# Layer 2's rows by expert: one scatter of every row, or a gather block by block through an index table

## What is computed

```python
xn = layernorm(x)                        # 2048 rows of 512
# attention: in each of the 512 columns l the 8 batches attend to each other
q = transpose(xn, (2, 0, 1))             # (l, batch, position c)
s = xn + transpose back(softmax(q q^T / sqrt(256)) q)
# mixture of experts: 8 experts, 2 per row, F = 800
probs = softmax(xn @ gate_w.T)
top_vals, top_idx = top_k(probs, 2); top_vals /= sum(top_vals)
h1, h3 = xn @ w1[e].T, xn @ w3[e].T
y = sum over the two experts of top_vals * ((silu(h1) * h3) @ w2[e].T)
x = x + s * silu(y)
```

## Time and profile before

| | us |
|---|---|
| median of 3 runs | 1500.8 (1498.28 to 1501.86) |
| the profiled execution | 1501.16, its span 1499.2 |
| PE busy | 1349.1 (90%) |
| DVE busy | 699.4 (47%) |
| ACT busy | 565.9 (38%) |
| GpSimd busy | 615.0 (41%) |
| attention of layer 1 | about 167 to 760 |
| across_batch | about 761 to 875.5 |
| experts | 875.6 to about 1445 |
| combine | about 1446 to the end |

### The profile page before, as it was taken

How to read it: one execution, slowest core, us unless ns; L and a number is a source line. 1 busy time by engine, 2 the same in 40 slices (tenths; PEclk the granted TensorE clock), 3 DMA queues, 4 the chain that set the end, 5 groups by cost and what they waited for, 6 DMA issues and landing times. The chain is left out here.

```text
span 1499.2 us, 24968 instructions
## 1 busy us (share of the span) xinstructions
PE 1349.1 (90%) x7870; PEld 1149.3 (77%) x7871; DVE 699.4 (47%) x1617; ACT 565.9 (38%) x1775; POOL 615.0 (41%) x516
## 2 busy tenths in 40 slices
PE   6989899999999999999877579999999999999940
PEld 6934487878787878888547469999999999999930
DVE  6352376666676766666447332223222222232237
ACT  3421276655556656666534221212212111122124
POOL 0020155444444545454325445172662617451135
PEclk9889999999999999999878689999999999999985
DMA  8035720000000000000015566273772728555247
GB/s 290 1 84 143 277 93 15 15 14 14 14 14 14 14 25 17 14 14 15 7 58 177 195 225 187 99 247 109 238 243 96 268 72 289 171 169 182 72 126 258
DMA packets 67068, 171.47 MB, mean 114 GB/s; under 512 B 6448, under 2 KB 15040, under 8 KB 66704
## 3 DMA queue, kind: packets, MB, share of 16 engines
q0 software_dynamic: 25776, 98.73, 19.9%
q1 hardware_dynamic: 35632, 61.95, 12.9%
q10 hardware_dynamic: 5616, 10.23, 1.9%
HBM read 125.26 MB, written 45.61 MB: 114 GB/s over the span
## 5 line engine op out<-in xcount | busy, mean ns | idle before, releaser
L1681 PE MATMUL bank<-expert_weights,rows_t 128*128 x1872 | 359.4, 347 | 1.8 <-DVE rows_t L1613 1.6
L1681 PEld LDWEIGHTS bank<-expert_weights,rows_t 128*128 128x128 f32 x1872 | 340.8, 189 | 5.8 <-issue 2.6
L958 ACT ACTIVATE room<-bank,room 128x256 f32<-128x256 f32 (+1 forms) x512 | 208.9, 415 | 114.0 <-DVE room L891 113.9
L986 POOL TENSOR_TENSOR room<-room 128x1024 f32<-128x1024 f32 (+1 forms) x128 | 187.9, 1468 | 120.1 <-DVE room L868 120.1
L742 PE MATMUL bank<-room 96*128 (+2 forms) x1024 | 189.1, 327 | 0.0
L1625 DVE TENSOR_TENSOR x_keep<-x_keep,bank 128x400 f32<-128x400 f32 x78 | 44.5, 571 | 304.2 <-ACT x_keep L1568 302.9
L1093 POOL TENSOR_TENSOR expert_weights<-x_keep,expert_weights 128x1600 fp32r<-128x1600 f32 (+2 forms) x49 | 160.2, 3270 | 54.9 <-DMA expert_weights<-w 54.6
L742 PEld LDWEIGHTS bank<-room 96*128 96x128 f32 x1024 | 159.1, 191 | 13.7 <-issue 0.4
L1704 PE MATMUL bank<-expert_weights,act_t 128*128 x702 | 165.6, 389 | 1.0 <-ACT act_t L1573 1.0
L993 POOL TENSOR_TENSOR room<-room 128x256 f32<-128x256 f32 x128 | 93.2, 728 | 173.5 <-DVE room L932 172.2
L1704 PEld LDWEIGHTS bank<-expert_weights,act_t 128*128 128x128 f32 x702 | 131.5, 188 | 25.6 <-issue 1.3
(11 more groups left out here) (231 smaller groups left out, 1773.4 us busy)
## 6 DMA issues: line engine op xcount, KB each, us to landing
x_keep<-w POOLq DMA_DIRECT2D x28, 800.0 KB, 5.0
expert_weights<-w POOLq DMA_DIRECT2D x28, 800.0 KB, 6.5
x_keep<-w POOLq DMA_DIRECT2D x14, 768.0 KB, 6.0
expert_weights<-w POOLq DMA_DIRECT2D x14, 768.0 KB, 7.7
rows_by_expert<-room SPq DMA_DIRECT2D x1, 9984.0 KB, 29.0
x_keep<-rows_by_expert SPq DMA_DIRECT2D x39, 256.0 KB, 4.0
results_by_row<-x_keep ACTq DMA_DIRECT2D x39, 256.0 KB, 4.6
room<-wo SPq DMA_DIRECT2D x16, 512.0 KB, 5.8
```

What stands on the lines that cost most here:

```text
L958: last = sc.activation(Pr[:, m % 4, hh, 0:w], scores_bank(m)[:, w * hh:w * hh + w], ACT.Exp, bias=nb[:, par, hh:hh + 1], accum_out=sm[:, p ...
L986: g.tensor_tensor(pr, pr, rs[:, one[1] % 2].unsqueeze(2).broadcast_to([P, 4, w]), ALU.mult).then_inc(normed, 1)
L1681: last = mm(psum(2 * hf + w)[:, 0:HF], xgT[:, par, of_x, P * k:P * k + P], W[:, ds(off + (of_w * SLOT + (k * 2 + w) * FF + hf * HF), HF)], ...
```

## The change

- xs is no longer filled with zeros, and the 32 scatters go. Instead, SP stores the 16 normalised tiles to a new DRAM tensor `rows_normalised` (xn), each as soon as it is ready.
- A table `s.index` is made that says for each place (128 of a block, 39 blocks) which row belongs there. DVE makes one-hot matrices of each pair's place in its block (`place_hit`, 32 x 128 columns) and of its block (`block_hit`, 32 x 39); they lie in X, whose rows are stored by then. `block_hit` multiplied by the row's number in its tile (on ACT) and by the tile's number (on DVE) is `named`. PE adds 32 products of the two, after round 5 of the attention. Places without a row get row 0.
- GpSimd gathers blocks 0 to 3 through the table, into X, and stores them to xs, at the end of `across_batch`. Blocks 4 to 38 it gathers, two in a step, in the first 18 of its 49 weight steps of `experts`, into a buffer of two blocks (`passing`), and stores them from there. SP loads the blocks from xs as before, waiting for those stores.
- The first expert's weights: three raw buffers instead of two, SP loads chunks 0 to 2 at once, the stores of xn behind them and chunks 3 to 6 behind those. The high parts of chunks 0 to 2 are brought by GpSimd's own loads; ACT makes those of 3 to 6 before the attention's rounds, chunk 3's before the router's exp. GpSimd makes the low parts 0 to 3 before the slots and 5 and 6 after them, DVE that of 4. Nothing of it is left for `experts`.
- The logits' four parts are added by 16 transposes and two reductions in place of 16 products. The tables of the blocks are made in round 5. GpSimd clears the 46 semaphores of `first_stage` at the start of `attention`.

```diff
@@ attention
         def _(pool):
-            nc.gpsimd.memset(zeros, 0.0).then_inc(s.zeros_ready, 1)
+            for of_first_stage in s.done_with:
+                pool.sem_clear(of_first_stage)
...
-            sp.wait_ge(s.zeros_ready, 1)
-            sp.dma_start(s.xs.rearrange("(n p) h -> p n h", p=P),
-                         zeros.unsqueeze(1).broadcast_to([P, NBLK, D])).then_inc(s.blank, 16)
@@ across_batch, SP
+            def keep_rows(t):
+                sp.wait_ge(xn_ready, t + 1)
+                sp.dma_start(s.xn[P * t:P * t + P, :], X[:, t]).then_inc(xn_stored, 16)
+
+            for c in range(3):
+                bring_chunk(sp, s, 0, c, raw[:, c % 3]).then_inc(s.raw0_in[c % 3], 16)
+            for t in range(NT):
+                keep_rows(t)
+            for c in range(3, NCH):
+                sp.wait_ge(pool_low, c - 2)
+                bring_chunk(sp, s, 0, c, raw[:, c % 3]).then_inc(s.raw0_in[c % 3], 16)
@@ across_batch, GpSimd
+            for c in DMA_HIGH:
+                at, rows, n = CHUNKS[c]
+                bring_chunk(pool, s, 0, c, s.W[:, at:at + n]).then_inc(high0_in[c], 16)
...
-            pool.wait_ge(s.blank, 16)
             pool.wait_ge(slots_ready, 1)
-            for t in range(NT):
-                for k in range(2):
-                    nc.gpsimd.indirect_dma_start(
-                        out=xs, out_offset=bass.IndirectOffsetOnAxis(ap=s.slots[:, t, k:k + 1], axis=0),
-                        in_=X[:, t], in_offset=None).then_inc(sorted_, 16)
-            pool.wait_ge(sorted_, 16 * 2 * NT)
+            for c in (5, 6):
+                pool.wait_ge(first_high, c - len(DMA_HIGH) + 1)
+                low_of(s, c, raw_of(c), 0).then_inc(pool_low, 1)
+            pool.wait_ge(index_steps, 7)
+            for b in range(4):
+                gather_rows(s, b, X[:, 8 + b])
+            pool.wait_ge(s.rows_got, 16 * 4)
+            for b in (0, 2):
+                keep_blocks(s, b, X[:, 8 + b:10 + b])
+            pool.wait_ge(s.rows_there, 16 * 2)
@@ across_batch, ACT
-            high_of(0)
+            high_of(3)
             act.wait_ge(p_ex, 1)
             sc.activation(p, p, ACT.Exp).then_inc(p_exd, 1)
-            high_of(1)
+            high_of(4)
+            high_of(5)
+            high_of(6)
@@ across_batch, DVE, in the rounds
+                if r == 0:
+                    find_blocks()
+                if r == 1:
+                    name_tiles()
+                if 1 <= r < 5:
+                    find_places(r - 1)
+                if r == 5:
+                    write_index()
+                    block_tables()
@@ across_batch, PE
+            def index():
+
+                pe.wait_ge(own_named, 1)
+                pe.wait_ge(index_steps, 6)
+                for i in range(2 * NT):
+                    last = mm(psum(7)[:, 0:2 * NBLK].rearrange("p (w b) -> p w b", w=2), place_hit[:, i], named[:, i],
+                              start=(i == 0), stop=(i == 2 * NT - 1))
+                last.then_inc(indexed, 1)
@@ experts, GpSimd
-            for c in range(KT_PER_D + 1, NCH):
-                at, rows, n = CHUNKS[c]
-                low_of(s, c, s.raw0[0:rows, c % 2, 0:n], 0).then_inc(first_w2, 1)
-
...
             for j in range((E - 1) * NCH):
                 e, c = 1 + j // NCH, j % NCH
                 more = j + 1 < (E - 1) * NCH
+                blocks = range(4 + 2 * j, min(6 + 2 * j, NBLK))
+                if blocks:
+                    pool.wait_ge(s.rows_there, 16 * (2 + j))
+                    for b in blocks:
+                        gather_rows(s, b, passing[:, b % 2])
                 if more:
                     bring_raw(j + 1)
...
                 low_of(s, c, stage[0:rows, j % 2, 0:n], e % 2 * 2 * SLOT).then_inc(s.converted, 1)
+                if blocks:
+                    pool.wait_ge(s.rows_got, 16 * blocks[-1] + 16)
+                    keep_blocks(s, blocks[0], passing[:, 0:len(blocks)])
                 if more and c + 1 == NCH:
                     bring_high(j + 1)
@@ experts, SP
+            for b in range(NBLK):
+                sp.wait_ge(s.rows_there, 16 * max(2, b // 2 + 1))
+                if b >= 2:
+                    sp.wait_ge(x_turned, b - 1)
+                load(b, b % 2)
```

181 lines of the change are left out of this document (116 added, 65 removed).

## The result

The changed kernel took 1543.8 us (median of 4 runs, 1541.2 to 1549.2), the kernel before 1499.6 beside it: a ratio of 1.030 (95% interval 1.028 to 1.032). It is slower by 44 us; the forecast was 1543.

The account below looks back on a forecast made before the run. Bound by engines waiting for instructions behind the scatters (25.9 us lost), then PE's expert blocks with weights just in time. 1501.2 - 20.4 (router, attention) + 0.2 + 61.7 (late weights, slow clock) = 1542.7, so 1543; range 1512 to 1572.

Parts of the forecast that it names:

- Step 1: Layer 2's router and attention: scatters gone saves 25.9 us, DVE's table work off the stage's end 2.0; gain 27.9.
- Steps 2 and 3: Router: queued transfers delay chunk 3 and the exp, +3 us; GpSimd's low parts collide with DVE in round 0, +2.
- Step 4: Attention rounds: index work mostly hidden on DVE, +1 us (0 to 5), plus PE's 32 small products, +1.5.
- 5 zero fill, clears: Start of first attention: dropping the zero fill gains nothing; GpSimd's clearing of 46 semaphores costs 0.2 us (0 to 1).
- Step 6: Expert stage: weights of experts 1, 2, 3 late by 12.1, 25.5, 17.3 us, sum 54.9; slow clock 6.8; together +61.7.
- p: Expert stage: length of a GpSimd chunk step with gathers, 12.6 us (10.9 to 14) instead of 5.95.
- S: Start of the expert stage, from which the prediction counted when expert 1's weights are whole and wanted.
- B: Expert stage: stores land almost at once, step near 8 us, only expert 3 late; 1487 us, chance 0.06.
- C: Router and attention: instruction waits stay, as other transfers replace the scatters; 1553 to 1569 us, say 1562; chance 0.11.
- D: Expert stage: an in-between case, chunk step between 9.5 and 10 us, a wash at 1501 us; chance 0.03.

Follow-up runs that it names:

- b3_no_scatters: The kernel before without its 32 scatters, so the experts work on zeros: 1474.8 us, beside 1500.1 for the kernel before.
- a3_in_gaps: The changed kernel with row gathers moved to where GpSimd has time, fitted to this input's block counts, same bytes: 1489.3 us, beside 1478.7 for the kernel before.
- a1_three_buffers: The changed kernel with a third passing buffer, so no step begins by waiting for the store just issued: 1514.1 us, beside 1478.7 for the kernel before.
- b4: The kernel before with its 32 scatters paced, at most two in flight: 1497.1 us, beside 1500.1 for the kernel before.
- b5: The kernel before with its 32 scatters paced by pairs, two to four in flight: 1487.2 us, beside 1500.2 for the kernel before.
- a4_low_later: The changed kernel with GpSimd's low parts of chunks 0 to 3 waiting for VectorE's mask copies: 1552.9 us, beside 1478.7 for the kernel before.
- a6: a3_in_gaps with ScalarE taking the router's exponential before it converts chunk 3: 1490.0 us, beside 1500.2 for the kernel before.
- a7: a3_in_gaps with both edits, GpSimd's low parts later and the exponential before chunk 3: 1486.1 us, beside 1478.4 for the kernel before.

## Why the prediction was right, point by point

| step | predicted | measured | by |
|---|---|---|---|
| 1 scatters gone | -25.9 | -24.4 | stage of b3_no_scatters, 90.4 for 114.8 |
| 1 tables off the end | -2.0 | -1.6 | last addition to row load, 0.8 for 2.4 |
| 2, 3 up to round 2 | +5 | +5.2 | round 2 of PE starts 51.7 us into the stage; 46.6 in b3 |
| 4 index work | +2.5 | +7.2 | round 2 to last addition 48.6 us; 41.4 in b3 |
| router and attention | -20.4 | -13.6 | |
| 5 zero fill, clears | +0.2 | within the scatter | starts of across_batch |
| 6 stalls | +54.9 | +53.4 | 3.9, 27.7, 21.9 |
| 6 slow clock | +6.8 | +6.6 | 6.19 + 7.08 + 7.24 - 3 x 4.63 |
| first row load | 0 | +3.8 | 7.75 us from SP's issue to PE, 3.93 before |

**The direction.** Right, by the step it rested on: the wait at the head of GpSimd's chunk step. The step p was put at 12.6 us and measured 12.2 and 13.4. a3_in_gaps shows that the 60 us come from where GpSimd's gathers, stores and waits stand, not from their bytes, and a1_three_buffers that the wait is the larger part.

**The number.** That 1543 met a median of 1543.8 within 1 us is partly luck. The sum was made against the profiled execution and had 41.5 us more than it; between the two profiled executions it is 48.0, with 6.8 us missing in the router and attention and 3.8 in the first row load, and against it the stalls 1.5 us less than forecast and `across_batch` starting 1.9 us earlier. The profiled execution of the changed kernel happened to lie 5.4 us over its median, and a second measurement of that kernel had a median of 1548.2.

**Step 1** held within 1.5 us, and 1.4 of that is the slower start of round 2, which lasted 7.39 us in b3 and 5.98 in the kernel before (807.38 to 813.36). That the "remote" waits come with the scatters is borne out by b3, b4 and b5. That the engines wait for their own instructions there is still a reading. For it, in the kernel before PE too pauses eight times between 826 and 838 us for 0.2 to 4.0 us put down to "issue". But the profile names no releaser, and the last instruction transfer that it records in that stretch, at 842.0 us, lies 7.8 us before the end of ScalarE's long wait. The Trainium skill ("Runtime: NRT & Kernel Launch", Instruction fetch mechanics) says that a sequencer fetches its own instructions over a DMA queue and that the cost is mostly hidden; if these waits are fetches, the trace of the kernel before has 24.5 us that were not hidden, and b4_paced, with two scatters in flight, none.

**Steps 2 and 3** came out at their sum, 5.2 for 5. Of this, 3.3 us are the exponential. The prediction named one cause, chunk 3 behind 9.9 MB of transfers, at 788.5 to 796 us; it was converted at 790.01, but it had been issued only at 783.69. What the step missed is the second cause beside it, GpSimd's subtractions over VectorE's normalisations. In round 0 a subtraction held a small operation of VectorE (803.92 us, L1425) for 2.90 us instead of 0.17, where 2 were taken. The Trainium skill ("GPSIMD Engine Reference", 1. Specifications) has the two engines contend when VectorE has two SBUF inputs or is in a two-port mode. The operations that were held here have one tensor as input, with scalars per partition, so by that rule it must have been the two-port mode; whether they ran in it, no row tells.

**Step 4** is the term that was mis-sized: 7.2 us for 2.5. The single durations were about right or even high (two of 1248 columns took 1.46 and 1.45 us, four of 1024 took 1.22 each, for 1.7 and 1.4 taken; PE's 32 products 1.34 for 1.5). Wrong was the cover: "each leaves 1.5" of a round's 5.35 us. VectorE's work in a round is a chain with PE and ScalarE, so a piece that stands in front of the next round's first reduction is not hidden by the idle time behind it. Three pieces, 4.4 us together, stood in front of one such reduction, at 818.70: the subtraction of chunk 4, which stays on VectorE, and two of the index operations.

```profile
814.52 1.75 DVE L1437 TENSOR_TENSOR expert_weights<-first_raw,expert_weights 128x1536 fp32r<-128x1536 f32 x1
816.19 1.45 DVE L1375 TENSOR_TENSOR x_keep<-x_keep,room 128x1248 bf16<-128x1248 bf16 x1
817.56 1.22 DVE L1382 TENSOR_TENSOR x_keep<-room,x_keep 128x1024 bf16<-128x1024 f32 x1
```

In b3, where a subtraction stands alone in a round, the round keeps its 5.35 us. Rounds 2 and 3 of the changed kernel lasted 7.18 and 9.52 us, against 7.39 and 5.35 in b3, as the scores of PE show:

```profile
810.66 1.06 PE L1499 MATMUL bank<-room 128*128 128x128 f32 x4
...
817.84 0.61 PE L1499 MATMUL bank<-room 128*128 128x128 f32 x4
...
827.36 0.61 PE L1499 MATMUL bank<-room 128*128 128x128 f32 x4
```

Round 3 alone gives 4.2 us of it, of which 1.5 are PE's messages at a granted clock of 0.52, after two pauses of 1.1 and 1.2 us (16 products in 3.57 us instead of 2.03); the round with PE's index products gives 1.2, and the one in which VectorE wrote the index and the block tables 1.5; the rest lies in the two half rounds at the end. The tables' 2 us, booked as a gain at the end, were in part paid back here.

**Step 6** came out right in sum with errors that cancel. Expert 1 was late by 3.9 us, not 12.1: it was whole at S + 82.4 instead of S + 87.5 (the first subtraction 1 us earlier, six steps 0.4 shorter each, the last one shorter by the rest), and wanted at S + 79.0 instead of S + 75.4, because the first rows came 3.8 us later. This was not in the sum. SP's first row load now follows its last 1 MB store of attention by 0.75 us instead of 2.37, so its 256 KB may wait behind that store; but in a1_three_buffers the same store stands the same 0.75 us ahead, and PE had its rows after 4.35 us. The cause stays open. Experts 2 and 3 were late by 27.7 and 21.9 instead of 25.5 and 17.3: the steps of expert 2 were 13.4 us and the three with gathers of expert 3 13.1, not 12.6. The landing of a 512 KB store was taken as 4.6 us; it took 3.1, 4.4 and 7.4 (least, median, longest). The Trainium skill ("DMA: Bandwidth & Descriptors", Anatomy of one DMA) would have it at an estimate of 3.2 us; that is near the least of them, and the median is near the 4.6 of the row from the same surroundings.

**Rivals.** B (the stores land at once) is excluded by the landings. C needed "remote" waits in the new kernel; it has none. D needed a step between 9.5 and 10 us; it was 12.2 and 13.4.

**The size against the kernel before.** The 1.03 holds beside a kernel before of 1500 us. Where that one takes 1478 us, a4_low_later, the changed kernel with one wait more, is at 1.048. The changed kernel itself was never run there. The prediction could not see this, since its one profile showed one of the two.

## What to carry to other kernels

Before a transfer is given to an engine that also prepares weights, write down the engine's step with every wait in it: here a wait for a landing cost 65.2 us over 15 steps, and everything behind it in order paid. Put the wait a step after the issue, or in a stretch in which the engine waits anyway (a3_in_gaps: 53 us of stalls gone with the same bytes). Ask of each added operation on a half-busy engine what stands behind it in the same round: idle time after it is no cover. Where one event has two late feeders, mend both before judging either, as a4, a6 and a7 show; and read more than one profile, since one of the two feeders was late in some executions only.

## What was not expected of the hardware

- Engines stand idle with no releaser in the program, by the likeliest reading for their own instructions, while GpSimd's indirect scatters run: 24.5 us of ScalarE when none of the 32 is held back (30.7 and 20.7 in two more profiles), 8.1 with up to four in flight, none with two. Pacing a kernel's scatters alone gave 13 us (1487.2 for 1500.2).
- The kernel with 32 scatters takes 1500 us in some groups of runs and 1478 in others, within 0.5% of its median inside a group, even on the same chip. Why is open.
- GpSimd's subtractions of 1600 columns stretched 16 one-tensor operations of VectorE from 10.3 to between 13.6 and 20.3 us, where they ran beside them; a subtraction of 1536 columns stretched one operation of 4 columns from 0.17 to 2.90 us.
